# Two layers of attention and feed-forward on one core: experts and router in one PSUM bank, three banks for maxima, chains cut into pieces, experts' rows built later

## The chip, the cores and the metric

One core of a Trainium2 chip runs the whole program. TensorE (PE), VectorE (DVE), ScalarE (ACT), GpSimd (POOL) and SyncE (SP, which here issues nearly all DMAs) each run their own list of instructions in order and wait for one another by semaphores. The metric is the device time of one execution in microseconds (us).

## The reference

The input is four sequences ("batches" in the kernel) of 512 tokens by 128. Two layers are computed, each an attention and a feed-forward part with a residual sum and a layer norm behind each.

- First attention: 16 heads of 8, each split into two half heads with a softmax of their own; `a = a1 - lam * a2`, out = `a @ v`, an RMS norm, then `@ wo`.
- First feed-forward: `silu(gate) * up`, then down, where every matmul's inputs are quantised to FP4 in blocks of 16 (block maximum / 6 as scale).
- Second attention: 16 query heads and 4 key heads of 64 with rotary positions, causal.
- Second feed-forward: a router picks one of 8 experts for each token; the expert is `relu(x @ W1 + b1) @ W2 + b2`, scaled by the router's weight.

## The kernel before

The four batches are pipelined. `attention1(r)` is the second attention of batch r, and `overlap(r)` runs three things beside each other: the first attention of batch r+1, the first feed-forward of batch r, and the experts of batch r-1. The order is start, overlap(-1), attention1(-1), overlap(0), attention1(0), overlap(1), and so on to overlap(4). In overlap(3) and overlap(4) there is no first attention left; `alone(i)` says so of the experts of batches 2 and 3.

The order of the work is written out by hand. An overlap walks over slots (s, c) with c from 0 to 3, and in each slot every engine does the same list: scores of the first attention, maxima, feed-forward, experts. The tables at the top (`UP`, `DOWN1`, `SORTED_TURN`, `HID_TURN`, `DOWN`, `O0_TURN`) say which piece stands in which slot. Every engine's list is fixed, so a wait holds all that stands behind it on that engine.

The first attention has two passes. In the first, PE computes two tiles of scores per slot into banks for maxima, and DVE reduces each (L895) and frees the bank. This pass runs 13 slots ahead of the second (`A_LEAD`). When a group of 16 maxima is there, POOL splits it into three parts, PE transposes them (L1416), DVE copies the row (L901), and SP sends it into three rows of `qst` (`max_row0`, L412). In the second pass PE computes two score tiles (L1435), which include the maxima through these rows, ACT takes the exponentials (L1160), and PE multiplies by the values (L1452). The scores of slots (s, 0) with even s wait for the row of group s / 2.

PSUM has eight banks. Banks 0 and 1 hold scores, 2 and 3 maxima, 4 the first attention's output, 7 the feed-forward and transposes. Banks 5 and 6 are added to scores and maxima in overlap(-1) and overlap(0), and are the experts' and the router's in overlap(1) and overlap(2).

The experts' stream: layer norm (`centre`, `scale`), transposes, router, `place_tokens` (which slot each token goes to, and which expert each of 11 tiles has), a scatter to HBM by POOL (L567), a fetch of the sorted rows by SP (L420) beside the experts' weights (L429), transposes (L1328), then for each tile up (L1346), relu (L1117), down (L1356) and a copy (L1122); a store, a gather by POOL (L573), and the last sum.

The weights are fetched from `expert_rows`, a copy in HBM that the kernel makes itself, with W1, W2 and b1 of an expert side by side; its nine DMAs are among `loads` (L357), which SP issues before overlap(-1). The quantisation of the feed-forward starts with `block_max`, `block_scale`, `over_scale` and `powers` on DVE and goes on with four steps on POOL (`quantise`, L546; L551 is the first, L560 the last). SP's order within an overlap is:

```
for g in range(NG):
    if r + 1 < BATCH:
        max_row0(r + 1, g)
    if 1 <= r:
        for j in WEIGHTS_AFTER.get(g, ()):
            fetch_expert(r - 1, j)      # j == 0 waits for tiles_ready
        if g == 1:
            fetch_sorted(r - 1)         # waits for the scatter
```

Of the kernel before, what the change touches and what calls it, by code (L numbers as in the profile page):

```python
# [17 lines left out]
P = 128  # L18
# [56 lines left out]
SLOTS = len(MAX_SLOT) + len(ROW_SLOT)  # L75

# [6 lines left out]
HID_TURN = {(5, 0): 0, (6, 0): 1, (7, 0): 2, (8, 0): 3}  # L83
HID_KEEP = {(5, 1): 0, (6, 1): 1, (7, 1): 2, (8, 1): 3}
DOWN = {(5, 2): 0, (6, 2): 1, (7, 2): 2, (8, 2): 3}
DOWN_KEEP = {(5, 3): 0, (6, 3): 1, (7, 3): 2, (8, 3): 3}
# [13 lines left out]
SORTED_TURN = {(3, 2): 0, (3, 3): 1, (4, 0): 2}  # L100
UP, DOWN_LAG, DOWN1 = {}, (2, 4), ({}, {})
for _n in range(2 * NTILE):
    _at = 17 + 43 * _n // (2 * NTILE)
    UP.setdefault((_at // 4, _at % 4), []).append((_n // 2, _n % 2))
    if _n % 2:
        for _lag, _table in zip(DOWN_LAG, DOWN1):
            _table[(_at + _lag) // 4, (_at + _lag) % 4] = _n // 2
# [5 lines left out]

def expert_banks(i, j):

    return (5, 6, 6) if not alone(i) else (2 * (j % 2), 2 * (j % 2) + 1, 5 + j % 2)
# [31 lines left out]
def banks0(r):  # L148

    return {-1: ((0, 1, 5), (2, 3, 6)), 0: ((0, 1, 6), (2, 3, 5))}.get(r, ((0, 1), (2, 3)))  # L150


def build(nc, x, w_qkv, wo, lq1, lq2, lk1, lk2, norm_w, w_gate, w_up, w_down,
# [8 lines left out]
    with ExitStack() as ctx:  # L162
# [127 lines left out]
        first_in, ffn_in, qk_in, weights_in = sem("first_in"), sem("ffn_in"), sem("qk_in"), sem("weights_in")  # L290
        setup_act, setup_pe, setup_dve, setup_pool = sem("setup_act"), sem("setup_pe"), sem("setup_dve"), sem("setup_pool")
# [52 lines left out]
        def _(sp):  # L344
# [8 lines left out]
            for i, v in enumerate((lq1, lk1, lq2, lk2)):  # L353
# [9 lines left out]
                (expert_rows[:, :, 0:FF1], W1),  # L363
                (sorted_x.rearrange("(t p) d -> p t d", p=P), nothing.rearrange("p (t d) -> p t d", t=NTILE)),
                (b2_sb[:, :], b2),
            ]
            for c in range(FF1 // P):
                loads.append((expert_rows[:, :, FF1 + E * c:FF1 + E * (c + 1)], W2.rearrange("e (c p) d -> c e p d", p=P)[c]))
                loads.append((expert_rows[:, :, WROW - FF1 // P + c:WROW - FF1 // P + c + 1],
                              b1.rearrange("e (c p a) -> c e p a", p=P, a=1)[c]))  # L370
# [110 lines left out]
        def _(pool):  # L481
# [64 lines left out]
            def quantise(a, c, n, done):  # L546
# [29 lines left out]
            def overlap(r):  # L576
# [4 lines left out]
                for g in range(NG):  # L581
# [4 lines left out]
                    if hidden and g in (2, 3):  # L586
                        if g == 2:
                            pool.wait_ge(hs_ready, r + 1)
                        next(rounds)
                        next(rounds)  # L590
# [3 lines left out]
            def turn(k, nx, v, rounds):  # L594

                if k < BATCH and 25 <= v < 29:
                    if v == 25:
# [33 lines left out]
        def _(dve):  # L631
# [125 lines left out]

            def over_scale(src, a, n, at=0):
# [6 lines left out]
            def place_tokens(i):  # L765

                count = ps[:, 5, NT * NE + NT * NE:NT * NE + NT * NE + NE]
                ranks = ps[:, 5, NT * NE:2 * NT * NE].rearrange("p (t n) -> p t n", t=NT)
# [4 lines left out]
                dve.wait_ge(ranks_ready, i + 1)  # L773
                step(dve.tensor_tensor(over, count.rearrange("p (e a) -> p e a", a=1).broadcast_to([P, NE, NT]),
                                       full_at.rearrange("p (a m) -> p a m", a=1).broadcast_to([P, NE, NT]), ALU.is_gt)); settle()
                step(dve.tensor_reduce(n_tiles, over, AX, ALU.add)); settle()
                step(dve.tensor_tensor(under, along(n_tiles, NE), tiles_under, ALU.mult)); settle()
                step(dve.tensor_reduce(base, under, AX, ALU.add)); settle()
                step(dve.tensor_tensor(rank_at, ranks, along(base, NT), ALU.add)); settle()
                step(dve.tensor_tensor(rank_at, rank_at, OH, ALU.mult)); settle()  # L780
                step(dve.tensor_reduce(slot_f, rank_at, AX, ALU.add)); settle()
                dve.tensor_copy(slot, slot_f).then_inc(slots_ready, 1)
                step(dve.scalar_tensor_tensor(ends, n_tiles, float(P), base, ALU.mult, ALU.add)); settle()
                step(dve.tensor_tensor(past, along(ends, NTILE), tile_at.rearrange("p (t a) -> p t a", a=1).broadcast_to([P, NTILE, NE]),
                                       ALU.is_le)); settle()
                step(dve.tensor_reduce(tile_f, past, AX, ALU.add)); settle()
                dve.tensor_scalar(tile_expert, tile_f, NE - 1.0, None, ALU.min).then_inc(tiles_ready, 1)

            def experts_stream(s, c, i):

                if (s, c) == (-1, 0):
# [3 lines left out]
                    dve.tensor_tensor(ZC[:, :, :], X[:, :, :], tiles(5), ALU.add).then_inc(att1_sum, 1)  # L795
                    dve.wait_ge(att1_sum, i + 1)
# [5 lines left out]
                if (s, c) == (0, 2):  # L802
                    dve.wait_ge(xc_turned, i + 1)
                    dve.tensor_copy(xTC[:, :], ps[:, 5, :]).then_inc(xTC_ready, 1)
                    centre(XP, bnC, mvC, varC)
                if (s, c) == (1, 0):
                    dve.wait_ge(logits_ready, i + 1)
                    step(dve.tensor_tensor(L, ps[:, 5, 0:NT * NE].rearrange("p (t n) -> p t n", t=NT), every(br_sb[:, :]), ALU.add)); settle()
                    step(dve.tensor_reduce(top, L, AX, ALU.max)); settle()
                    step(dve.tensor_tensor(IS, L, each(top), ALU.is_equal))  # L810
                    dve.tensor_tensor(OG, L, each(top), ALU.subtract).then_inc(lc_ready, 1); settle()
# [12 lines left out]
                if (s, c) == (2, 2):  # L824
                    dve.wait_ge(oh_turned, i + 1)
                    dve.tensor_copy(ohT, ps[0:NE, 5, :]).then_inc(ohT_ready, 1)
                    dve.wait_ge(oh_ready, i + 1)
                if (s, c) in SORTED_TURN:
# [3 lines left out]
                    dve.tensor_scalar(xsT[:, 4 * P * b:4 * P * b + w], ps[:, 5 + b % 2, 0:w], lng[:, 0:1], lng[:, 1:2],  # L832
# [21 lines left out]
            def ffn_stream(s, c, r):  # L854
# [4 lines left out]
                if (s, c) in ((0, 1), (0, 2)):  # L859
                    if c == 1:  # L860
                        dve.wait_ge(hid_done, NT * (r + 1))
                        dve.wait_ge(xq_ready, r + 1)
                    block_max(part(hl, c - 1), 704, 44 * (c - 1))
                if (s, c) == (0, 3):
                    block_scale(1408)
                if (s, c) in ((1, 0), (1, 1)):
                    settle()
                    step(over_scale(part(hl, c), part(ha, c), 704, 44 * c))
# [784 lines left out]
```

## Time and profile before

| | |
|---|---|
| median of 3 runs | 1362.13 us (1359.47 to 1363.06) |
| profiled execution | 1364.12 us, span from first to last instruction 1362.3 us |
| granted TensorE clock, mean | 0.823 |
| PE busy | 1040.2 us (76%) |
| DVE busy | 778.9 us (57%) |
| ACT busy | 646.9 us (47%) |
| POOL busy | 451.1 us (33%) |

Times within the profile count from the span's start. Busy shares are means over stages that differ; a stage is read by its own window. "idle before <-X" in a row is the time for which the engine stood idle ahead of that instruction, and what ended it. The granted clock is a share of 2.4 GHz.

### The profile page before, as it was taken

Reading aid. Unit: us, or ns where it says so; the run is one execution under the profiler, and the core shown is the slowest. Engines: PE = TensorE matmul, PEld = TensorE weight load, DVE = VectorE, ACT = ScalarE, POOL = GpSimd, SP = SyncE. Lnnn points to the kernel's source line nnn. Section 1 sums busy time; section 2 is a strip of 40 time slices with the busy share of each in tenths; the row PEclk is TensorE's granted clock in tenths of the full one; section 3 lists DMA queues with packets and bytes.
Section 4 is the critical chain, followed back from the end, with each engine's and each line's share of the span. In section 5 each row is a group of like instructions: output and inputs, shape, how many; then the busy total and the mean of one; then the engine's idle time right before and its main releaser. Section 6 shows DMA issues by size and latency. Waiting matters only on the chain. (4 is left out here: it accounts for less than half of the span.)

```text
span 1362.3 us, 20051 instructions
## 1 busy us (share of the span) xinstructions
PE 1040.2 (76%) x7121; PEld 538.4 (40%) x7121; DVE 778.9 (57%) x1809; ACT 646.9 (47%) x1581; POOL 451.1 (33%) x520
## 2 busy tenths in 40 slices
PE   2458837788998867789889866889888836799845
PEld 1012321233455432444445441444445526445534
DVE  4458447774777566463677656564487541376431
ACT  1057712577266233577266423577347513246414
POOL 3000020400677203200477503200376622278411
PEclk7569965789999665889999875799999967899957
DMA  5710030000012003100103002200100014100042
GB/s 140 188 30 3 10 101 0 2 2 10 1 47 55 0 1 122 49 17 23 40 1 102 1 1 77 94 18 17 38 1 1 1 56 144 37 1 1 1 168 68
DMA packets 54305, 56.83 MB, mean 42 GB/s; under 512 B 13688, under 2 KB 46016, under 8 KB 53440
## 3 DMA queue, kind: packets, MB, share of 16 engines
q1 hardware_dynamic: 53184, 53.47, 13.6%
q0 software_dynamic: 1024, 2.10, 0.5%
q8 instruction: 57, 0.93, 0.3%
q14 instruction: 40, 0.33, 0.1%
HBM read 43.16 MB, written 16.20 MB: 44 GB/s over the span
## 5 line engine op out<-in xcount | busy, mean ns | idle before, releaser
L895 DVE TENSOR_REDUCE mx<-ps 128x1 f32<-128x512 f32 x512 | 323.7, 684 | 156.5 <-PE ps L1410 153.4
L1160 ACT ACTIVATE PROB<-ps 128x512 f32<-128x512 f32 x512 | 276.1, 600 | 196.3 <-PE ps L1435 193.7
L538 POOL TENSOR_SCALAR PROB<-PROB,rsum 128x128 f32<-128x128 f32 (+3 forms) x224 | 229.0, 1035 | 62.0 <-DVE rsum L1023 61.6
L1202 ACT ACTIVATE PROB<-ps,mx 128x128 f32<-128x128 f32 (+3 forms) x256 | 133.1, 526 | 156.5 <-DVE mx L1018 154.3
L1410 PE MATMUL ps<-kst,qst 24*128 24x512 bf16 x512 | 170.0, 478 | 39.8 <-DVE mx L895 25.7
L1435 PE MATMUL ps<-qst,kst 27*128 27x512 bf16 x512 | 143.4, 445 | 53.5 <-DMA qst<-mrow 31.1
L519 POOL CAST mparts<-mx 128x16 bf16<-128x16 f32 x32 | 6.3, 197 | 526.7 <-DVE mx L895 526.7
L1452 PE MATMUL ps<-PROB,v 128*32 128x256 f32 x2048 | 175.4, 434 | 3.0 <-ACT OREG L1169 2.7
L1018 DVE TENSOR_REDUCE mx<-ps 128x1 f32<-128x128 f32 (+3 forms) x256 | 113.1, 483 | 72.9 <-PE ps L1497 72.9
L1514 PE MATMUL ps<-cst,PROB 128*128 128x128 f32 x640 | 114.1, 301 | 32.5 <-POOL PROB L538 11.4
L1494 PE MATMUL ps<-MREG,QREG 64*128 64x384 f32 (+3 forms) x512 | 107.4, 497 | 0.0
L1435 PEld LDWEIGHTS ps<-qst,kst 27*128 27x128 bf16 x512 | 32.8, 93 | 185.1 <-ACT PROB L1160 86.0
L1514 PEld LDWEIGHTS ps<-cst,PROB 128*128 128x128 f32 x640 | 75.2, 149 | 61.4 <-issue 22.9
L1117 ACT ACTIVATE MREG<-ps,wexp 128x128 f32<-128x128 f32 x176 | 53.9, 368 | 84.7 <-PE ps L1346 84.7
L1011 DVE SCALAR_TENSOR_TENSOR RREG<-ps,bqk,rope_sb 128x512 f32<-128x512 f32 x96 | 67.7, 746 | 21.1 <-PE ps L1479 21.1
L1524 PE MATMUL ps<-PROB,MREG 128*64 128x256 f32 (+3 forms) x512 | 77.5, 445 | 0.7 <-DVE PROB L1031 0.7
L1410 PEld LDWEIGHTS ps<-kst,qst 24*128 24x128 bf16 x512 | 37.5, 94 | 99.3 <-DVE mx L895 77.9
L1217 ACT COPY PROB<-ps 128x128 f32<-128x128 f32 (+3 forms) x128 | 54.4, 425 | 43.3 <-PE ps L1514 43.1
L1452 PEld LDWEIGHTS ps<-PROB,v 128*32 128x32 f32 x2048 | 47.6, 115 | 58.8 <-issue 41.0
L1031 DVE COPY PROB<-ps 128x128 f32<-128x128 f32 (+3 forms) x128 | 60.8, 475 | 11.3 <-PE ps L1514 10.7
L1479 PE MATMUL ps<-xT,wq_sb 128*128 128x512 f32 x128 | 61.2, 605 | 0.9 <-DVE MREG L1045 0.9
L1346 PE MATMUL ps<-PROB,wexp 128*128 128x128 f32 x352 | 60.1, 308 | 1.9 <-DVE PROB L832 1.9
(210 smaller groups left out, 1376.8 us busy)
## 6 DMA issues: line engine op xcount, KB each, us to landing
wexp<-expert_rows SPq DMA_DIRECT2D x44, 514.0 KB, 4.8
qk_terms<-RREG SPq DMA_DIRECT2D x48, 128.0 KB, 2.1
kst<-qk_terms SPq DMA_DIRECT2D x16, 192.0 KB
qst<-qk_terms SPq DMA_DIRECT2D x16, 192.0 KB
RREG<-sorted_x SPq DMA_DIRECT2D x4, 704.0 KB, 4.7
sorted_y<-RREG SPq DMA_DIRECT2D x4, 704.0 KB, 3.9
expert_rows<-in_L_ffn_W_dram SPq DMA_DIRECT2D x1, 2048.0 KB
expert_rows<-in_L_ffn_W_dram SPq DMA_DIRECT2D x4, 512.0 KB
```

The source lines that it names most:

```text
L538: pool.tensor_scalar(tile, tile, rsum1[:, 2 * v + half:2 * v + half + 1], None, ALU.mult).then_inc(scaled1, 1)
L895: dve.tensor_reduce(mx0[:, ga % 2, col:col + 1], ps[:, max_banks[MAX_SLOT[n] % len(max_banks)], :], AX, ALU.max, negate=True).then_inc(slo ...
L1011: dve.scalar_tensor_tensor(ropeT[:, i % 2, u], ps[:, banks[u], :], bqk[:, u, c:c + 1], rope_sb[:, u], ALU.add, ALU.mult).then_inc(rope_rea ...
L1018: dve.tensor_reduce(mx1[:, col:col + 1], ps[:, a1_bank(v, half), 0:P * (v % 4 + 1)], AX, ALU.max, negate=True).then_inc(max1_done, 1)
L1160: act.activation(prob0[:, s % 2, q % 4, q % 8 // 4], ps[:, s0_banks[q % len(s0_banks)], :], ACT.Exp, scale=float(HD0) ** -0.5).then_inc(ex ...
L1202: act.activation(prob1[:, half, at:at + w], ps[:, a1_bank(v, half), 0:w], ACT.Exp, bias=mx1[:, col:col + 1], accum_out=sum1[:, col:col + 1 ...
L1410: pe.matmul(ps[:, max_banks[at % nm], :], qst[rows, n // 16, P * qt:P * (qt + 1)], kst[rows, n // 16, :], start=True, stop=True).then_inc( ...
L1435: pe.matmul(ps[:, s0_banks[q % ns], :], kst[rows, g, P * kt:P * (kt + 1)], qst[rows, g, :], start=True, stop=True).then_inc(s0_ready, 1)
L1452: ins = pe.matmul(ps[32 * j:32 * j + 32, 4, qs], v0[:, kt, 4 * j + m // 4, :], prob0[:, m % 2, j, u // 2, qs], start=(m % 2 == 0 and u == ...
L1494: pe.matmul(dst[i], qT[half(i), w, P * qt:P * (qt + 1)], k1[half(i), g, 0:n], start=True, stop=False)
L1514: ins = pe.transpose(ps[:, 4 + i, P * kt:P * (kt + 1)], prob1[:, i, at + P * kt:at + P * (kt + 1)], ident)
L1524: ins = pe.matmul(ps[64 * h:64 * h + 64, 6, P * kt:T], v1[:, kt, D1 * (w // 2):D1 * (w // 2 + 1)], probT[:, w % 2, h, (TSTEP + P) * kt:(TS ...
```

## The change

In overlap(1) and overlap(2) the router and the experts use bank 6 alone, and bank 5 is a third bank for the maxima from the 19th on (`LEAD`). An expert tile takes three slots: both halves of up and half of the relus in the first, the other relus in the second, down and the copy in the third. The sorted rows' transposes go through bank 6 one group after another. The DVE chains of the router and of the quantisation, which stood in slots (0,1) to (2,2), are cut into pieces, at most one in a slot, up to (4,3); what hangs on them moves (sorted transposes from (3,2) to (5,0), first tile from (4,1) to (6,2), feed-forward transposes from (5,0) to (6,2), the transpose of X from (10,0) to (14,2)). The first of POOL's four quantisation steps becomes a DVE step (`shifts`). The nine DMAs that build `expert_rows` are issued after the term loads of overlap(-1), with a semaphore of their own that SP awaits before overlap(1). The loads of the second attention's q and k weights go behind the first term loads.

```diff
-HID_TURN = {(5, 0): 0, (6, 0): 1, (7, 0): 2, (8, 0): 3}
+HID_TURN = {(6, 2): 0, (7, 2): 1, (8, 2): 2, (9, 2): 3}
...
-SORTED_TURN = {(3, 2): 0, (3, 3): 1, (4, 0): 2}
-UP, DOWN_LAG, DOWN1 = {}, (2, 4), ({}, {})
+SORTED_TURN = {(5, 0): 0, (5, 2): 1, (6, 0): 2}
+UP, DOWN1 = {}, {}
 for _n in range(2 * NTILE):
-    _at = 17 + 43 * _n // (2 * NTILE)
+    _at = 25 + 35 * _n // (2 * NTILE)
...
+def tile_at_slot(s, c, lead):
+    n = 4 * s + c - lead - 26
+    return n // 3 if n >= 0 and n % 3 == 0 and n // 3 < NTILE else None
...
+def max_bank(k, at):
+    if k >= 2 and at < LEAD:
+        return 2 + at % 2
+    return (2, 3, 6 if k == 0 else 5)[at % 3]
...
-            for dst, src in qk_loads:
-                sp.dma_start(dst, src, allow_slow_non_contiguous=True).then_inc(qk_in, 16)
             n_loads[:] = [len(ffn_loads), len(qk_loads), len(loads)]
             store_parts(0)
             load_terms(0)
+            for dst, src in qk_loads:
+                sp.dma_start(dst, src, allow_slow_non_contiguous=True).then_inc(qk_in, 16)
...
                 if r == 1:
                     sp.wait_ge(weights_in, 16 * n_loads[2])
+                    sp.wait_ge(experts_in, 16 * len(expert_loads))
...
                     fetch_again(r + 2)
+                if r == -1:
+                    for dst, src in expert_loads:
+                        sp.dma_start(dst, src, allow_slow_non_contiguous=True).then_inc(experts_in, 16)
...
-                step(pool.tensor_scalar(c, c, 1.0, 1.5 * 2.0 ** 22, ALU.max, ALU.mult))
-                yield
-                settle()
                 step(pool.tensor_tensor(a, a, c, ALU.add))
...
+            def shifts(c):
+                return dve.tensor_scalar(c, c, 1.0, 1.5 * 2.0 ** 22, ALU.max, ALU.mult)
...
-                if (s, c) == (1, 2):
+                if (s, c) == (2, 1):
                     scale(XP, ZC, mvC, stC, stdC, 3 * i + 2, lnC)
-                    place_tokens(i)
-                if (s, c) == (1, 3):
+                if (s, c) in ((2, 3), (3, 1), (3, 3)):
+                    place_tokens(i, 2 * s + c // 2 - 5)
+                if (s, c) == (4, 1):
...
-                if (s, c) in ((0, 1), (0, 2)):
+                if (s, c) in ((0, 0), (0, 2)):
...
-                if (s, c) in ((1, 2), (1, 3)):
+                if (s, c) in ((2, 2), (3, 0)):
                     settle()
-                    ins = powers(part(ha, c - 2), part(hc, c - 2))
+                    step(powers(part(ha, s - 2), part(hc, s - 2)))
+                if (s, c) in ((3, 2), (4, 0)):
+                    settle()
+                    ins = shifts(part(hc, s - 3))
...
+                    j = tile_at_slot(s, c, 0)
+                    if j is not None:
+                        n = NTILE * i + j
+                        if j == 0:
+                            pe.wait_ge(xe_ready, 3 * (i + 1))
+                        else:
+                            pe.wait_ge(y_kept, n)
                         pe.wait_ge(wexp_in[n % RING], 16 * (n // RING + 1))
...
+                        up(i, j, 0, 6, 0)
+                        up(i, j, 1, 6, 0).then_inc(up_ready, 2)
+                    j = tile_at_slot(s, c, 2)
+                    if j is not None:
+                        n = NTILE * i + j
+                        pe.wait_ge(relu_done, 4 * (n + 1))
+                        down(n, ps[:, 6, 0:P]).then_inc(down1, 1)
...
-                if (s, c) == (10, 0):
+                if (s, c) == (14, 2):
                     pe.wait_ge(lnB, 2 * r + 2)
+                    if r + 1 < BATCH:
+                        pe.wait_ge(o0_kept, NG * (r + 1) + 6)
                     transpose_tiles(X, 7, x_turned)
```

`place_tokens` keeps its instructions; its piece 1 ends with the slots and its piece 2 with the tiles' experts.

## Rows read from the trace of the kernel before

**Rows 1.** Windows: stretch and length, engines' busy us, clock, DMA share, GB/s.

```profile
0.00:80.20 80.20, 22.99 (x52) 7.84 (x52) 30.99 (x59) 4.68 (x9) 12.50 (x44) 0.60 0.63 151
25.90:28.80 2.90, 2.08 (x9) 1.65 (x9) 2.69 (x12) 1.44 (x4) 0.00 (x0) 0.50 0.40 136
40.00:54.00 14.00, 11.97 (x22) 2.01 (x22) 12.11 (x21) 0.00 (x0) 0.83 (x4) 0.50 1.03 293
54.00:80.20 26.20, 2.20 (x5) 0.51 (x5) 3.72 (x7) 0.00 (x0) 0.00 (x0) 0.50 0.43 86
492.70:654.00 161.30, 132.21 (x1048) 63.62 (x1049) 88.03 (x190) 98.81 (x209) 27.14 (x40) 0.79 0.15 49
```

**Rows 2.** SP in order of time, the start: start, us, what.

```profile
10.65 0.43 SPq L458 DMA_DIRECT2D wq_sb<-in_L_attn_Wq_dram  x1
...
19.04 7.67 SPq L401 DMA_DIRECT2D qk_terms<-RREG  x12
28.24 1.54 SPq L410 DMA_DIRECT2D kst<-qk_terms  x4
...
73.94 5.18 SPq L415 DMA_DIRECT2D qst<-mrow  x3
```

**Rows 3.** PE and DVE in order of time, the start.

```profile
41.20 0.61 PE L1410 MATMUL ps<-kst,qst 24*128 24x512 bf16 x3 [13.11 <-DMA qst<-qk_terms]
...
55.05 0.20 DVE L901 COPY mrow<-ps 48x128 bf16<-48x128 bf16 x1
...
80.25 0.60 PE L1435 MATMUL ps<-qst,kst 27*128 27x512 bf16 x2 [23.67 <-DMA qst<-mrow]
```

**Rows 4.** Windows of overlap(1): slots (0,0), (4,0), (6,2) on.

```profile
492.70:541.90 49.20, 34.41 (x189) 10.78 (x189) 35.73 (x89) 22.13 (x38) 13.89 (x14) 0.50 0.21 66
541.90:569.50 27.60, 21.20 (x177) 11.68 (x173) 13.15 (x23) 14.79 (x35) 6.53 (x6) 0.81 0.25 86
569.50:646.00 76.50, 68.70 (x606) 36.49 (x607) 38.16 (x78) 57.41 (x131) 3.32 (x16) 0.96 0.06 18
```

**Rows 5.** Waits of PE in overlap(1): us in total, times, longest.

```profile
PE ps L1416 <- DVE mx L895: 7.0, 6, 2.3
```

**Rows 6.** POOL and PE in order of time, overlap(0) at slot (5,0).

```profile
259.32 3.15 POOL L557 TENSOR_TENSOR QREG<-QREG 128x1408 f32<-128x1408 f32 x1
262.54 2.58 POOL L560 TENSOR_TENSOR QREG<-QREG,q_sc 128x1408 f32<-128x1408 f32 x1
265.18 0.90 PE L1385 MATMUL ps<-cst,QREG 128*128 128x128 f32 x3 [5.78 <-POOL QREG L560]
```

**Rows 7.** DMA issues on the page: count, KB each, median us to landing.

```profile
wexp<-expert_rows SPq DMA_DIRECT2D x44, 514.0 KB, 4.8
```

**Rows 8.** All engines in order of time, before overlap(0)'s first score.

```profile
188.19 1.55 SPq L410 DMA_DIRECT2D kst<-qk_terms  x4
...
190.94 1.94 POOL L551 TENSOR_SCALAR ZB<-ZB 128x512 f32<-128x512 f32 x1 [9.71 <-DVE ZB L763]
...
224.81 1.79 SPq L415 DMA_DIRECT2D qst<-mrow  x3
...
227.74 0.60 PE L1435 MATMUL ps<-qst,kst 27*128 27x512 bf16 x2 [1.62 <-DMA qst<-mrow]
```

**Rows 9.** DVE and SP in order of time, overlap(1).

```profile
516.52 0.17 DVE L787 TENSOR_SCALAR tile_expert<-tile_f 128x11 int32<-128x11 f32 x1
517.81 3.02 SPq L429 DMA_DIRECT2D wexp<-expert_rows  x3
...
533.02 1.80 SPq L415 DMA_DIRECT2D qst<-mrow  x3
538.57 2.57 SPq L429 DMA_DIRECT2D wexp<-expert_rows  x3
```

**Rows 10.** PE in order of time: after overlap(1), and in overlap(3).

```profile
659.02 2.90 PE L1479 MATMUL ps<-xT,wk_sb 128*128 128x512 f32 x3 [4.17 <-DVE oall L916]
...
1156.54 0.93 PE L1291 MATMUL ps<-cst,X 128*128 128x128 f32 x4 [2.35 <-DVE X L737]
```

More of the change, by code:

```diff
@@ L145, in a1_bank, with score_banks, max_before @@
     return 2 * (v % 2) + half
-def banks0(r):
-    return {-1: ((0, 1, 5), (2, 3, 6)), 0: ((0, 1, 6), (2, 3, 5))}.get(r, ((0, 1), (2, 3)))
+def score_banks(r):
+    return {-1: (0, 1, 5), 0: (0, 1, 6)}.get(r, (0, 1))
+def max_bank(k, at):
+    if k >= 2 and at < LEAD:
+        return 2 + at % 2
+    return (2, 3, 6 if k == 0 else 5)[at % 3]
+def max_before(k, at):
+    for n in range(at - 1, -1, -1):
+        if max_bank(k, n) == max_bank(k, at):
+            return n
+    return None
 def build(nc, x, w_qkv, wo, lq1, lq2, lk1, lk2, norm_w, w_gate, w_up, w_down,
@@ L589, in overlap @@
                         next(rounds)
+                    if hidden and g == 3:
                         next(rounds)
@@ L594, in turn @@
             def turn(k, nx, v, rounds):
-                if k < BATCH and 25 <= v < 29:
-                    if v == 25:
+                if k < BATCH and 26 <= v < 29:
+                    if v == 26:
                         pool.wait_ge(xs_ready, k + 1)
@@ L778, in place_tokens @@
[L778 to L787, printed above, removed]
+                if piece == 0:
+                    dve.wait_ge(ranks_ready, i + 1)
+                    step(dve.tensor_tensor(over, count.rearrange("p (e a) -> p e a", a=1).broadcast_to([P, NE, NT]),
+                                           full_at.rearrange("p (a m) -> p a m", a=1).broadcast_to([P, NE, NT]), ALU.is_gt)); settle()
+                    step(dve.tensor_reduce(n_tiles, over, AX, ALU.add)); settle()
+                    step(dve.tensor_tensor(under, along(n_tiles, NE), tiles_under, ALU.mult)); settle()
+                    step(dve.tensor_reduce(base, under, AX, ALU.add))
+                elif piece == 1:
+                    settle()
+                    step(dve.tensor_tensor(rank_at, ranks, along(base, NT), ALU.add)); settle()
+                    step(dve.tensor_tensor(rank_at, rank_at, OH, ALU.mult)); settle()
+                    step(dve.tensor_reduce(slot_f, rank_at, AX, ALU.add)); settle()
+                    dve.tensor_copy(slot, slot_f).then_inc(slots_ready, 1)
+                else:
+                    settle()
+                    step(dve.scalar_tensor_tensor(ends, n_tiles, float(P), base, ALU.mult, ALU.add)); settle()
+                    step(dve.tensor_tensor(past, along(ends, NTILE), tile_at.rearrange("p (t a) -> p t a", a=1).broadcast_to([P, NTILE, NE]),
+                                           ALU.is_le)); settle()
+                    step(dve.tensor_reduce(tile_f, past, AX, ALU.add)); settle()
+                    dve.tensor_scalar(tile_expert, tile_f, NE - 1.0, None, ALU.min).then_inc(tiles_ready, 1)
@@ L985, in input0 @@
                     step(over_scale(rows(XA[:, :, :]), XQ[:, :], T)); settle()
-                    powers(XQ[:, :], rows(ZB[:, :, :])).then_inc(xs_ready, 1)
+                    step(powers(XQ[:, :], rows(ZB[:, :, :])))
+                if v == 25:
+                    settle()
+                    shifts(rows(ZB[:, :, :])).then_inc(xs_ready, 1)
             def turn(k, nx, v):
@@ L1292, in transpose_tiles, with up, down @@
                 ins.then_inc(done, 1)
+            def up(i, j, h, bank, at):
+                for f in (2 * h, 2 * h + 1):
+                    ins = pe.matmul(ps[:, bank, P * f - at:P * f - at + P], wexp[:, (NTILE * i + j) % RING, P * f:P * (f + 1)],
+                                    xsT[:, P * j:P * (j + 1)], start=True, stop=True)
+                return ins
+            def down(n, dst):
+                for f in range(4):
+                    ins = pe.matmul(dst, hE[:, n % 2, f, :], wexp[:, n % RING, FF1 + E * f:FF1 + E * (f + 1)],
+                                    start=(f == 0), stop=(f == 3))
+                return ins
             def experts_stream(s, c, i):
-                if (s, c) == (0, 1):
+                if (s, c) == (0, 0):
                     pe.wait_ge(lnC, 3 * i + 1)
-                    transpose_tiles(XP, 5, xc_turned)
+                    transpose_tiles(XP, RB, xc_turned)
                 if (s, c) == (0, 3):
@@ L1324, in experts_stream @@
                         pe.wait_ge(xs_in, 16 * (i + 1))
-                    if b == 2:
-                        pe.wait_ge(xe_ready, 3 * i + 1)
+                    if b and not alone(i) or b == 2:
+                        pe.wait_ge(xe_ready, 3 * i + (1 if alone(i) else b))
                     for t in range(4 * b, min(4 * b + 4, NTILE)):
-                        ins = pe.transpose(ps[:, 5 + b % 2, P * (t % 4):P * (t % 4) + P], xs[:, t], ident)
+                        ins = pe.transpose(ps[:, sorted_bank(i, b), P * (t % 4):P * (t % 4) + P], xs[:, t], ident)
@@ L1462, in overlap @@
                             if g == 0 and r >= 0:
+                                pe.wait_ge(ffn_sum, NT * (r + 1))
+                            if g == 6 and r >= 0:
                                 pe.wait_ge(xT_ready, 2 * r + 2)
```

211 lines of the change are left out of this document (113 added, 98 removed).

## The prediction

> **What bounds it now.** The views were read in this order: busy time by stages, SP's queue, PE's order of time, the waits. The chain of waits is of little use here: it breaks off at 1156 us. No engine is full; the time lies in waits of in-order queues, each with one place.
>
> The first place is the start. [rows 1] show 80.2 us with PE busy for 23.0. SP issues the twelve stores of the q and k parts from 19.04 and loads them again from 28.24; then come the other loads and the experts' rows, and only at 73.94 can it issue the first row of maxima [rows 2]. DVE had copied that row at 55.05; PE waits 23.67 us for it, until 80.25 [rows 3].
>
> The second place is overlap(1), 161.3 us for 64 slots with DVE busy for 88.0 [rows 1]; overlap(2) repeats it. [rows 4] split it: slots (0,0) to (3,3) take 49.2 us at a granted clock of 0.50, which is 1.2 GHz, with DVE busy 35.7; (4,0) to (6,1) take 27.6, (6,2) to (15,1) 76.5 with PE busy 68.7. The first stretch is long because DVE's chains stand in clumps between maxima that PE needs freed. In the second, slot (5,0) waits for POOL's quantisation, as it does in overlap(0) for 5.78 us [rows 6].
>
> **Part 1, the start.** Thirteen loads leave the place ahead of the stores. These begin at 10.65 instead of 19.04 at the earliest [rows 2], a little later because POOL must have made the parts, so the term loads, which took 13.0 us (28.24 to 41.20, [rows 2, 3]), land about 7 us earlier, at 34. But the thirteen now stand behind them, and DVE's set-up needs them before its first maximum. Their issue (8.4 us) hides behind the term loads; their landing does not: 0.7 MB at the 293 GB/s of [rows 1] is 2.5, small pieces and latency add 3, so 40. Set-up is 2.7 [rows 1]; maxima start at 43, or at 46 if SP is held at the small pieces. I take 44.4 against 41.9 before: the 7 us are lost to the next thing that is late. The row's copy follows 13.2 later, at 57.6. SP has about twelve loads left and is free by then; in overlap(0) a row issued at 224.81 was used at 227.74 [rows 8], 2.9. Scores begin at 60.5 instead of 80.25: **-19.7**, ends -23 (set-up hidden) and -16 (SP still held).
>
> **Part 2, the experts' rows later.** SP now issues them behind the term loads of the next batch and ahead of overlap(0)'s first row of maxima (224.81, [rows 8]). In times of before: those term loads land at 188.19 + 13.0 = 201.2. At the start the rest took from 41.20 to 80.25, 39.0, of which 2.4 MB of other loads are 8.2 at 293 GB/s [rows 1]: 30.9. So the row is in at 232.1 instead of 227.7, +4.4. Below: 0 (the copy runs beside the term loads); above: +11 (all 39). I take **+5**, near the sum and a little towards the middle. It swallows a small gain: POOL's first quantisation step of 1.94 us in the serial stretch before overlap(0) [rows 8] becomes a DVE step, bounded by 0.2 (mean of the set-up's, [rows 1]) and 1.94; I take 0.5, but it is SP that is late there.
>
> The trace moved 293 GB/s while large loads ran (40 to 54 us) and 86 while the experts' small pieces ran (54 to 80) [rows 1]. Beside these rows stands the Trainium skill, "DMA: Bandwidth & Descriptors", section Specifications: about 358 GB/s of HBM for a core. By it 4.2 MB read and as much written are an estimated 23.4 us, the row would land in time, and the sum would be 5 lower, 1318. The trace does not reach that figure.
>
> **Part 3, quantisation in the overlaps.** POOL's four steps become three, and their user moves from (5,0) to (6,2). POOL gets its flag at (4,0): 2 for that slot, 3.2 for the first step, which is of the kind of L557, then after the parts at (4,2) its last two, 3.15 and 2.58 [rows 6], with gaps about 12. (6,2) is ten slots on; eleven slots of the lead took 13.85 (41.20 to 55.05, [rows 3]), 1.26 each, so 12.6. The wait goes: -5.8 in overlap(0), and -0.7 for slots behind it that ran at 1.2 GHz; DVE, which is the limit there, has two steps more at 0.5: **-5.5**. Ends -8 and -2. If the cover of 0.6 is gone, it costs what POOL is late, 1 or 2.
>
> **Part 4, overlap(1) and (2), each.** PE may run a slot ahead of DVE with the third bank, and the row transposes (7.0 us of waits, [rows 5]) look a bank further back. With DVE's chains in pieces, slots (0,0) to (3,3) are bounded by DVE: 35.7 less 2.8 that moves past (4,0), plus 0.5 for a new step and 2.6 of gaps, 36 us. Alone that is -13. But SP's order is unchanged: behind the second row of maxima it waits for the tiles' experts, issues three expert loads, waits for the scatter, fetches the sorted rows, and only then sends the third row, which PE's score at (4,0) needs. Before, the experts were known at 516.69, 25 us ahead of (4,0). Now they are known at the end of (3,3). From there [rows 9]: 1.1 to SP's first issue, 2.0 to the third, 4.8 to its landing (the median, [rows 7]), and for the sorted rows and the row behind them the 5.55 from 533.02 to 538.57, less 1 that runs beside the weights: 12.5. Behind that score stand PE's maxima, so DVE and ACT stop too. 36 + 12.5 = 48.5 against 49.2: **-0.7**, ends -8 and +8.
>
> From (4,0) ten slots without POOL's wait, at 2.0 since the sorted rows now pass one bank after another: 20 against 27.6, -7.6. From (6,2) on PE is the limit [rows 4]: eleven tiles instead of about nine (2 x 2.3) and 1.5 of the first layer more, four row waits of 1 less: +2. The last tile's copy comes two slots earlier, and PE idles 4.17 before the next stage for want of it [rows 10]: -3. Together -9 each, **-18**; ends -17 and +3 each.
>
> **Part 5, the rest.** In overlap(3) PE no longer waits 2.35 amid the tiles [rows 10], POOL is a step earlier, the slots are known 1 later: **-3**, ends -6 and +2. Overlap(4) and the second attentions do the same work: **0**, ends -1 and +2.
>
> Sum: -19.7 + 5 - 5.5 - 18 - 3 = -41.2. The profiled execution took 1364.12 (span 1362.3), so 1322.9. It lies 2 us above the median of 1362.13; I say **1323**.
>
> **Rivals.** (a) *SP is not late at (4,0)*: the row, a few KB, passes the weights, or DVE's pieces end sooner. For it: at 533.02 the row shared the queue with the sorted rows and was not far behind them. Each overlap gains some 11 more: 1301. (b) *The overlaps gain nothing*: PE's own order holds the early slots (34.4 us of work in 49.2 at half clock, [rows 4]), and what is won from (4,0) on is lost in the denser tile slots. Without the -18: 1341. (c) *The stall only moves*: the experts' rows cost overlap(0) what they cost the start, 20 instead of 5: 1338. Against it: 23 us lie between the landing of the terms (201.2) and the row (224.81), which the start had not. (d) *Slower*: the queue of rows at (4,0) takes the place of the waits removed. If slots (0,0) to (3,3) do not shrink, the 12.5 come on top, and if the fourth row is held in the same way by the next three expert loads, another 7. Two overlaps at +19.5 with -19.7 + 5 - 5.5 - 3 make +16: 1380. It decides from 11.6 each. Against it: the fourth row is copied five slots after (4,0), by when three loads (2.0 + 4.8) are in.
>
> **Chances.** Forecast 0.52, (a) 0.17, (b) 0.16, (c) 0.09, (d) 0.06. The range takes the forecast's ends, (a) and (b): 1299 to 1346. About 0.3% is what a measurement of this kernel tells from no change. Faster: all but (d) and tails of (b) and (c), 0.91; within it 0.04; slower 0.05.
>
> **What would show it.** Right: the first score near 60 us, with no expert copy ahead of its row; overlap(0)'s first score some 5 us after its maxima allow; no first-layer transpose waiting for POOL; in overlap(1) one wait of PE of 10 us or more for a row of maxima, behind three expert loads. Wrong: overlap(1) above 160 us, or a first score after 70.

## The result, and the profile after

The changed kernel takes 1311.87 us (median of 4 runs, 1310.01 to 1315.45), the kernel before in the same comparison 1362.6 (4 runs, 1359.47 to 1363.25): a ratio of 0.9635 [0.9609, 0.9661]. 1323 was forecast, so the time by itself lies no nearer to the forecast than to rival (a), 1301; the trace has to tell them apart. The profiled execution took 1311.07, its span is 1309.3 and its mean granted clock 0.826 (before 0.823).

Where the 53.0 us of span went is read from marks that both kernels have (TensorE's first or last score of an overlap, the end of a second attention), in us from the span's start. The last column puts the prediction's terms against the stretches.

| mark | before | after | ahead by | this stretch | forecast |
|---|---|---|---|---|---|
| first score of overlap(-1) | 80.2 | 58.1 | 22.1 | -22.1 | -19.7 |
| first score of overlap(0) | 227.7 | 210.4 | 17.3 | +4.8 | +5 |
| last score of overlap(0) | 334.2 | 308.8 | 25.4 | -8.1 | -5.5 |
| first score of overlap(1) | 492.7 | 462.6 | 30.1 | -4.7 | 0 |
| first score of overlap(2) | 806.9 | 766.6 | 40.3 | -10.2 | -9 |
| end of attention1(2) | 1095.2 | 1043.1 | 52.1 | -11.8 | -9 |
| start of attention1(3) | 1181.0 | 1125.5 | 55.5 | -3.4 | -3 |
| end | 1362.3 | 1309.3 | 53.0 | +2.5 | 0 |

Windows of the kernel after, columns as in [rows 1]: the start up to the first score; then overlap(1) from the score at (0,0) to that at (3,3), from there to (4,0), from there to (6,2), and from (6,2) to the last score. The two lines between are from the time in which the experts' rows are copied.

```profile
0.00:58.10 58.10, 22.35 (x52) 7.30 (x52) 31.87 (x59) 4.68 (x9) 12.49 (x44) 0.63 0.53 136
...
172.00:182.00 10.00, 4.19 (x9) 2.26 (x10) 0.68 (x2) 2.33 (x3) 3.58 (x3) 0.50 0.97 246
182.00:204.50 22.50, 18.57 (x38) 5.17 (x37) 15.29 (x27) 2.67 (x4) 0.83 (x4) 0.50 0.51 118
...
462.60:495.10 32.50, 27.01 (x165) 8.26 (x165) 30.66 (x77) 20.91 (x36) 2.30 (x9) 0.50 0.00 1
495.10:510.00 14.90, 1.70 (x16) 0.37 (x12) 3.19 (x8) 1.10 (x3) 3.66 (x4) 0.50 0.58 173
510.00:529.30 19.30, 16.53 (x136) 5.25 (x136) 16.38 (x28) 10.76 (x21) 9.69 (x7) 0.74 0.29 89
529.30:608.20 78.90, 73.63 (x669) 40.66 (x665) 38.65 (x79) 61.40 (x147) 5.30 (x18) 0.96 0.14 44
```

The score at (3,3) comes 32.5 us into overlap(1), where it came at 46.7 before; DVE is busy for 30.7 of them, so it is nearly full. Then for 14.9 us hardly an engine works, so that (4,0) comes at 47.4, against the 49.2 of [rows 4]. The stretch from (4,0) to (6,2), which held POOL's wait, fell from 27.6 to 19.3. The timeline of the same kernel (start, us, engine, line; idle time before it in brackets) answers [rows 2, 3, 8 and 9]:

```profile
21.87 1.55 SPq L438 DMA_DIRECT2D kst<-qk_terms  x4
...
33.75 0.61 PE L1497 MATMUL ps<-kst,qst 24*128 24x512 bf16 x3 [6.23 <-DMA qst<-qk_terms]
...
39.07 0.69 DVE L734 TENSOR_SCALAR wq_sb<-wq_sb 128x1024 f32<-128x1024 f32 x1 [13.67 <-DMA bqk<-in_L_attn_bk_dram]
...
41.76 13.25 DVE L941 TENSOR_REDUCE mx<-ps 128x1 f32<-128x512 f32 x22
...
55.16 81.55 SPq L443 DMA_DIRECT2D qst<-mrow  x24
58.12 0.61 PE L1522 MATMUL ps<-qst,kst 27*128 27x512 bf16 x2 [1.66 <-DMA qst<-mrow]
...
171.98 2.96 SPq L508 DMA_DIRECT2D expert_rows<-in_L_ffn_W_dram  x2
174.99 11.01 SPq L508 DMA_DIRECT2D expert_rows<-in_L_ffn_b_dram  x1
...
203.85 0.21 DVE L947 COPY mrow<-ps 48x128 bf16<-48x128 bf16 x1
...
204.55 4.76 SPq L443 DMA_DIRECT2D qst<-mrow  x3
...
210.44 0.61 PE L1522 MATMUL ps<-qst,kst 27*128 27x512 bf16 x2 [5.06 <-DMA qst<-mrow]
...
498.07 0.32 DVE L825 TENSOR_SCALAR tile_expert<-tile_f 128x11 int32<-128x11 f32 x1
499.50 3.07 SPq L457 DMA_DIRECT2D wexp<-expert_rows  x3
502.62 0.43 SPq L448 DMA_DIRECT2D RREG<-sorted_x  x1
503.09 2.33 SPq L443 DMA_DIRECT2D qst<-mrow  x3
...
510.04 0.61 PE L1522 MATMUL ps<-qst,kst 27*128 27x512 bf16 x2 [13.24 <-DMA qst<-mrow]
```

The row of maxima now goes out at 55.16, as soon as DVE has copied it, and no copy of experts' rows stands ahead of it. In overlap(1) the forecast's one long wait is there: the row of slot (4,0) leaves at 503.09, behind three weights and the sorted rows. PE's waits (us in total, times, longest), in overlap(1) and then in overlap(3):

```profile
PE ps L1522 <- DMA qst<-mrow: 13.8, 2, 13.2
...
PE ps L1407 <- DMA RREG<-sorted_x: 11.8, 1, 11.8
```

### The profile page after: what moved, and what is told of

It reads as the page before. It is cut to its first block, busy times and chain, and to the rows that moved or that the text cites. A ratio compares the mean times of both kernels' runs of the same rounds, so it can differ in the third digit from the quotient of the medians.

```text
span 1309.3 us, 20064 instructions
## 1 busy us (share of the span) xinstructions
PE 1027.1 (78%) x7121; PEld 525.3 (40%) x7121; DVE 784.8 (60%) x1821; ACT 642.1 (49%) x1581; POOL 424.7 (32%) x512
## 4 chain that ended last, share of the span: by engine, by line
PE 54%; DVE 18%; ACT 9%; issue 8%; DMA 4%; SPq 3%; POOL 3%; POOLq 0%; ACTq 0%; DVEq 0%
PE ps L1539 9%; DVE mx L941 8%; PE ps L1568 7%; PE ps L1522 6%; PE ps L1583 5%; PE ps L1603 4%; PE ps L1613 4%; PE ps L1369 3%; ACT PROB L1227 3%; PE ps L1676 3%; PE ps L1456 2%; PE ps L1363 2%; DMA qst<-mrow 2%; PE ps L1497 2%; PE ps L1554 1%
## 5 line engine op out<-in xcount | busy, mean ns | idle before, releaser
L1497 PE MATMUL ps<-kst,qst 24*128 24x512 bf16 x512 | 158.3, 479 | 39.0 <-DVE mx L941 27.4
L1539 PE MATMUL ps<-PROB,v 128*32 128x256 f32 x2048 | 183.3, 451 | 3.0 <-ACT OREG L1236 2.6
L1603 PE MATMUL ps<-cst,PROB 128*128 128x128 f32 x640 | 113.3, 298 | 30.1 <-ACT PROB L1284 9.8
L1497 PEld LDWEIGHTS ps<-kst,qst 24*128 24x128 bf16 x512 | 34.1, 94 | 88.9 <-DVE mx L941 69.3
L1080 DVE COPY PROB<-ps 128x128 f32<-128x128 f32 (+3 forms) x128 | 60.8, 475 | 10.6 <-PE ps L1603 10.2
L962 DVE COPY oall<-ps 128x144 f32<-128x144 f32 x32 | 9.7, 303 | 95.5 <-PE ps L1554 95.5
```

What stands on the lines that cost most here:

```text
L1497: pe.matmul(ps[:, max_bank(k, at), :], qst[rows, n // 16, P * qt:P * (qt + 1)], kst[rows, n // 16, :], start=True, stop=True).then_inc(slo ...
L1539: ins = pe.matmul(ps[32 * j:32 * j + 32, 4, qs], v0[:, kt, 4 * j + m // 4, :], prob0[:, m % 2, j, u // 2, qs], start=(m % 2 == 0 and u == ...
L1603: ins = pe.transpose(ps[:, 4 + i, P * kt:P * (kt + 1)], prob1[:, i, at + P * kt:at + P * (kt + 1)], ident)
```

## Experiments

Medians are compared with 1311.9 of the changed kernel; the kernel before gave 1362.7, 1367.4 and 1363.5 beside the three sets. A kernel's runs spread over 4 to 10 us, so small effects are read from slots of the traces.

**The two parts of the start.** `qk_first` puts the q and k loads back:

```diff
+            for dst, src in qk_loads: ...
             store_parts(0)
             load_terms(0)
-            for dst, src in qk_loads: ...
```

> The changed kernel with the loads of the second attention's q and k weights put back ahead of the first stores. In the changed kernel the first terms land at 33.7 us, but DVE waits for these loads until 39.1 and its first maximum starts at 41.8, as it did before (41.89). Theory: moving the loads gained nothing, because DVE's set-up waits for them in place of the terms; the first maximum stays at 42 (+-1), the first score at 58, the time within 2 us of 1312. Rival: the earlier terms are worth their 7 us all the same (the row of maxima goes out into a less busy queue); then the first score comes at 65 and the time is 1319.

1310.2 us (ratio 0.9613 [0.9589, 0.9637]); the first score is at 58.4. The terms come at 41.4 again and nothing is lost. So this part of the change is worth nothing, as theory said: the first maximum waited for the terms before, and now it waits for the loads that were moved behind them.

`rows_early` issues `expert_loads` ahead of the loop over the overlaps again, instead of after `overlap(-1)`.

> The changed kernel with the nine copies that build the experts' rows put back ahead of overlap(-1). Theory (steps 1 and 2 of the prediction): SP is held by them until about 76, so the first score comes at about 79 instead of 58 (+21), and overlap(0)'s first row is no longer late, which gives back 5: 1328 (1323 to 1333). Rival: the stall only moves, and costs overlap(0) what it costs the start: 1312, with the first score of overlap(0) no later than now (210).

1327.6 us (0.9722 [0.9693, 0.9751]): 15.7 slower. The first row leaves at 76.25 and the first score is at 82.8 (+24.6); from the term loads of overlap(0) to its first score it takes 37.3 us (193.6 to 230.9) instead of 42.1 (168.3 to 210.4), 4.8 given back. The rival is out. The whole gain of the start is this one move, and within the changed kernel its price is the 5 that theory gave.

**What a wait at the start still costs.** `start2` moves DVE's set-up of the q and k weights (a wait and eleven steps) from ahead of the first maximum to slot (12,0) of overlap(-1), the k weights land in a place of their own meanwhile, and `expert_loads` go out behind overlap(0), ahead of `store_parts`:

```diff
-            dve.wait_ge(qk_in, 16 * n_loads[1])
...
+                    if r == -1 and (s, c) == (12, 0):
+                        set_up_qk()
...
+                    if r == 0:
+                        for dst, src in expert_loads: ...
...
-        wk_in = PROB[:, 7168:7424]
+        wk_in = QREG[:, 3584:3840]
```

> The changed kernel with two things moved: DVE's set-up of the second attention's q and k weights from ahead of the first maximum to slot (12,0) of overlap(-1), and the nine copies of the experts' rows from ahead of overlap(0) to behind it. Theory: the first maximum follows the terms at 33.8 instead of 41.8, so the first score comes at 50 (-8); overlap(0)'s first row is no longer behind the copies, -2.6 from there; 1301 (1298 to 1304). Rival 1: something else is late at the start (ACT's or PE's set-up, SP's other loads until 46.3 ahead of the row): first score at 54 or later, 1305. Rival 2: the copies now hold up the second attention or the next terms: nothing gained there, 1304.

1304.0 us (0.9543 [0.9516, 0.9570]). The first score came at 51.1, 7.0 earlier, so nothing else was late. From the term loads to overlap(0)'s first score it took 36.6 us instead of 42.1, and the copies held up nothing behind overlap(0): from its last score to overlap(1)'s first it took 155.7 us, within the 151.9 to 156.7 of the runs with the copies ahead of it, so the second rival is out. But overlap(-1) itself took 92.5 us to its last score instead of 88.5: at (12,0) the set-up holds up maxima, and 4 us went there: from (12,0) to (13,0) it took 9.4 us instead of 5.5 (see `best4`).

**SP's order in overlap(1) and (2).** `row_first` sends the third row before SP waits for the tiles' experts:

```diff
-WEIGHTS_AFTER = {1: (0, 1, 2), 2: (3, 4, 5), 3: (6, 7, 8), 5: (9,), 6: (10,)}
+WEIGHTS_AFTER = {2: (0, 1, 2), 3: (3, 4, 5), 4: (6, 7, 8), 5: (9,), 6: (10,)}
...
+                        if g == 2:
+                            fetch_sorted(r - 1)
                         for j in WEIGHTS_AFTER.get(g, ()):
                             fetch_expert(r - 1, j)
-                        if g == 1:
-                            fetch_sorted(r - 1)
```

> The changed kernel with SP's order changed in overlap(1) and (2): the third row of maxima goes out before SP waits for the tiles' experts; the sorted rows and the experts' weights follow it. Theory: PE's wait of 15 us at slot (4,0) is SP's order alone; it goes, some 4 us come back at (5,0), where the sorted rows are then late: 11 less in each of the two overlaps, 1290 (1286 to 1296). Rival 1: the wait only moves to (5,0), since scatter and fetch end when they did; 2 to 4 us in each, 1306. Rival 2: behind the wait the engines had work stored up that they then do faster; the slots after it run slower by as much without it, 1312.

1281.8 us (0.9392 [0.9368, 0.9415]): 30 less, where 22 were expected. Slot (4,0) comes at 34.1 us of overlap(1) instead of 47.4 and no wait appears at (5,0); 11.2 and 10.8 are left at the last score of overlap(1) and (2). So far theory, and both rivals are out. The other 8 lie where no row is sent: overlap(3) became 4.1 shorter (from the end of attention1(2) to the start of attention1(3), 78.3 instead of 82.4) and the last stretch 3.6. There only the sorted rows' place ahead of the weights can act. In waits of PE in this kernel, overlap(3) and then overlap(4):

```profile
PE ps L1407 <- DMA RREG<-sorted_x: 8.1, 1, 8.1
...
PE ps L1407 <- DMA RREG<-sorted_x: 8.9, 1, 8.9
```

They were 11.8 and 12.2. `row_only` keeps the order of weights and sorted rows (`fetch_sorted` stays behind the weights, both after g == 2) and moves the row alone:

> The changed kernel with the third row of maxima ahead of the wait for the tiles' experts as in the run with the row first, but the sorted rows behind the three weights as in the changed kernel. Theory: two effects are mixed in the 30 us of the row-first run. The row's own place is worth 11 in each of overlap(1) and (2); the sorted rows' place ahead of the weights is worth the rest in overlap(3) and (4), where no row is sent: there PE's wait for the sorted rows was 11.8 and 12.2 and became 8.1 and 8.9. So here 22 of the 30: 1290 (1286 to 1294), with the waits in overlap(3) and (4) at 12 again; in overlap(1) the sorted rows may be late by up to 3 at (5,0). Rival: the weights ahead of the sorted rows cost nothing, the 30 are the row's: 1282.

1295.0 us (0.9508 [0.9477, 0.9540]), 17 of the 30 and 1 us outside theory's range. The waits in overlap(3) and (4) are 11.4 and 12.1 again; in overlap(1) the sorted rows are 2.0 late for the transposes at (5,0), and the last scores of overlap(1) and (2) come 4.6 and 0.7 later than in `row_first`. The rival is out: the row is worth a little over half, the sorted rows' place the rest. How weights delay sorted rows is seen in overlap(3), in time, first of the kernel after:

```profile
1063.62 2.61 SPq L457 DMA_DIRECT2D wexp<-expert_rows  x3
1065.54 0.96 POOL L596 DMA_INDIRECT sorted_x<-ZC,slot  x1 [0.30 <-issue]
1071.71 0.38 SPq L448 DMA_DIRECT2D RREG<-sorted_x  x1
```

and of `row_first`:

```profile
1046.32 0.97 POOL L596 DMA_INDIRECT sorted_x<-ZC,slot  x1 [0.30 <-issue]
1048.57 0.36 SPq L448 DMA_DIRECT2D RREG<-sorted_x  x1
1049.95 1.51 SPq L457 DMA_DIRECT2D wexp<-expert_rows  x2
```

With three weights on the way SP saw the scatter land 6.2 us after POOL's last issue, without them 2.3; in overlap(4) it was 5.5 and 2.3.

**The third bank and the pieces.** `two_banks` sets `LEAD = SLOTS`.

> The changed kernel, in which the maxima of overlap(1) and (2) use banks 2 and 3 alone, all the way (the freed bank 5 stays empty for them). Theory: from (-1,0) on each maximum and each row transpose waits for the bank two places back instead of three; the slots up to (3,3) are bounded by DVE's chains and end 0 to 3 us later, and the row transposes behind them wait about 1 us more, five times: 3 to 8 in each overlap, 1323 (1316 to 1328). Rival: the pieces alone were enough and the third bank does nothing, since PE is held by SP at (4,0) and by its own work after it: 1312.

1323.3 us (0.9696 [0.9655, 0.9737]): 11.4 slower. In overlap(1) and (2) slot (3,3) comes 2.1 later, (4,0) 1.4 and 2.9, the last score 6.7 and 4.7. So in overlap(1) the third bank is worth most behind (4,0), in overlap(2) more than half of it ahead. Row transposes wait for a maximum again ([rows 5] has 7.0), in overlap(1):

```profile
PE ps L1503 <- DVE mx L941: 5.2, 6, 1.2
```

The rival is out.

`clumped` stands on `row_first`, so that SP's wait hides nothing, and puts the chains back to (0,1) to (2,2):

```diff
-                if (s, c) in ((2, 3), (3, 1), (3, 3)):
-                    place_tokens(i, 2 * s + c // 2 - 5)
+                if (s, c) == (1, 2): ...
+                    for piece in range(3):
+                        place_tokens(i, piece)
...
-                if (s, c) == (2, 0):
+                if (s, c) == (1, 1):
                     pe.wait_ge(oh16_ready, i + 1)
```

> The kernel with the row of maxima first (1281.8) with DVE's and ACT's chains of router and quantisation, and PE's router steps, back in the slots (0,1) to (2,2) in which they stood before; the third bank, the tables of the later slots and SP's order stay. Theory (step 4): the clumps are what made the slots up to (3,3) long; (3,3) comes at 40 to 46 us of overlap(1) instead of 32.5, and about 9 of it stays to the end of the overlap, twice: 1300 (1292 to 1308). Rival: the third bank carries the clumps, since PE may run a slot further ahead; (3,3) at 34, 1283.

1289.3 us (0.9439 [0.9418, 0.9460]): 7.5 slower than `row_first`. Slot (3,3) is at 37.1 and 38.5 in overlap(1) and (2): 4.6 and 5.9 later, between theory (7.5 to 13.5) and rival (1.5). The last scores come 2.4 and 4.4 later, where theory had 9 each. Theory's size was wrong. `clumped2` undoes both:

> The row-first kernel (1281.8) with the chains back in their old slots and the maxima of overlap(1) and (2) on two banks: what the two runs before undid one by one, undone together. Slot (3,3) came at 46.7 us in the kernel before, 32.5 in the changed one, 34.6 with two banks, 37.1 and 38.5 with the chains clumped. Theory: a bank more is what lets PE run on while DVE works on a clump; without both, (3,3) comes at 43 to 47, more than the sum of the two losses (39.2), and some 10 of it stays to the end of each overlap on top of the banks' 6: 1310 (1302 to 1318). Rival: they add, (3,3) at 39 to 41, 1300. The kernel before had router and experts in two banks, here they have one, so its 46.7 needn't come back whole.

1304.0 us (0.9577 [0.9543, 0.9611]). Slot (3,3) is at 41.6 in both overlaps: 9.1 later than in `row_first`, where the single losses are 2.1 and 4.6 to 5.9. So there is an interplay, but of 1 to 2 us, not the 4 to 8 that theory gave it: the slots come nearer to the rival. And 41.6 is not the 46.7 of the kernel before. The missing 5.1 are in that kernel's trace, at slot (3,2), where PE needed the sorted rows:

```profile
537.29 1.09 PE L1328 MATMUL ps<-cst,RREG 128*128 128x128 f32 x4 [5.05 <-DMA RREG<-sorted_x]
```

The change moved these transposes to (5,0). So of the 14.2 us by which (3,3) came earlier, 9.1 are chains and bank and 5.1 this wait. That split holds to about 1 us: up to (3,2) the kernel before was 1.1 ahead of `clumped2` (39.0 and 40.1), and from there to (3,3) it took 7.7 instead of 1.5, the wait and the transposes themselves.

**POOL's step.** `pool_back` gives `shifts` back to POOL, as the first of its four steps.

> The changed kernel with the first quantisation step back on POOL (4.94 us in an overlap, 1.94 in the attention before it) and the two DVE steps gone; the transposes that wait for it stay at slot (6,2). In the changed kernel POOL's last step ends at 249.4 us and the first of these transposes starts at 252.4: 3.0 us of slack in overlap(0). Theory (step 3): the 4.94 don't fit into it. The parts of the row behind the first step come 4.9 later and the last step at 254: overlap(0) loses 2 to 5, the stretch before it about 1, overlap(1) and (2), whose ten slots take 20 us, nothing: 1316 (1313 to 1319). Rival 1: moving the transposes to (6,2) alone cured the wait: 1312. Rival 2: POOL's step is what mattered and its wait comes back in each overlap: 1322 or more.

1316.7 us, against a slower kernel before (0.9638 [0.9602, 0.9674]), so the times alone don't tell it from the changed kernel. The trace does. POOL and PE's waits in overlap(0) of this kernel:

```profile
240.81 4.94 POOL L583 TENSOR_SCALAR QREG<-QREG 128x1408 f32<-128x1408 f32 x1 [8.21 <-DVE QREG L797]
...
249.78 0.22 POOL L554 TENSOR_TENSOR mparts<-mrem,mparts 128x16 bf16<-128x16 f32 x1
```

```profile
PE ps L1498 <- POOL mparts L554: 4.2, 1, 4.2
```

The long step holds back the parts of the next row, which end 37.8 us behind the overlap's first score (212.2) instead of 33.2 (243.6 and 210.4), and PE waits 4.2 us for them; (5,2) comes 3.0 later, the last score 2.4. Overlap(1) and (2) lose nothing, and neither does the stretch ahead of overlap(0) (41.6 us from the term loads to the first score, 42.1 in the changed kernel), where theory had 1. Otherwise theory holds; the wait is at the row of maxima rather than at the quantised tile.

**Together.** `best3` is `row_first` and `start2`:

> The row of maxima first, DVE's set-up late, the experts' rows behind overlap(0), all three on the changed kernel. Theory: the three stand in different stages and add: 1281.8 - 8 - 2.6 = 1271 (1267 to 1275). Rival: the copies behind overlap(0) run into the first attention's later loads and take back what they gave: 1274 to 1278.

1273.6 us (0.9309 [0.9284, 0.9333]), inside theory's range: the stages add. `best4` moves the set-up from (12,0) to (15,1), behind the last maximum:

> The row first, the experts' rows behind overlap(0), DVE's set-up late, but at slot (15,1) of overlap(-1), behind the last maximum, instead of (12,0), where it stood among maxima and that overlap became 4 us longer. Theory: the 4 come back: 1269.5 (1266 to 1273). Rival: overlap(-1) became longer because its granted clock fell at another time, not for the set-up's place: 1273.5.

1271.2 us (median of 6, 1266.6 to 1276.4; 0.9329 [0.9299, 0.9359]). Overlap(-1) takes 86.0 us to its last score instead of 92.1, in the one profile of each; but the medians differ by 2.4 only, and by the ratios not at all. The set-up's place is shown in the slots ((12,0) to (13,0) 5.5 instead of 9.4), not in the time. It is 41 us faster than the changed kernel and 92 faster than the one before.

## Why the prediction was right

**Part 1, right, and 2.4 too small.** -19.7 was forecast, -22.1 came. Maxima started at 41.8, not at 44.4: the loads landed at 39.1 instead of the 40 to 43 of the forecast; the row then took 3.2 from its copy, near the 2.9 of [rows 8]. The 3 us for small pieces and latency, which the forecast took from no row, came out: from PE's first maximum, which the terms released (33.75), to the landing it was 5.3, where 5.5 was forecast. What gave the gain is SP being free (`rows_early`); the loads' move gave 0 (`qk_first`), which is the forecast's own 7 us lost to the next late thing.

**Part 2, right in its mechanism; that its number fits is luck.** +5 was forecast and the stretch has +4.8, but only 2.6 of that lie where the late row acts. From the term loads to the first score it became 2.6 us longer (39.5 to 42.1). The first maximum came 0.8 sooner behind the term loads (16.0 instead of 16.8); the row's copy followed the first maximum as before (19.6); and from the copy to the score it took 6.6 instead of 3.2, because SP came to the row only at 204.55 and the row then landed behind the copies. In the kernel before these were

```profile
205.01 0.61 PE L1410 MATMUL ps<-kst,qst 24*128 24x512 bf16 x3
...
224.59 0.20 DVE L901 COPY mrow<-ps 48x128 bf16<-48x128 bf16 x1
```

and in the changed kernel

```profile
168.31 1.55 SPq L438 DMA_DIRECT2D kst<-qk_terms  x4
...
184.28 0.61 PE L1497 MATMUL ps<-kst,qst 24*128 24x512 bf16 x3
```

In all eight traces with the copies in this place it took 41.1 to 42.9, so against the kernel before they cost 1.6 to 3.3. Taking them out of the changed kernel gives back more, 4.8 (`rows_early`) to 5.5 (`start2`). What the DVE step in POOL's place gave (0.5 forecast) is not shown: with the step back on POOL, `pool_back`, the stretch took 41.6.

The other 2.2 were lost ahead of the term loads, where overlap(-1) took 88.5 us to its last score instead of 85.5. The forecast had no term there. The granted clock was 0.56 from 82 to 90 us and 1.00 at the same slots before (104 to 112), and with these slots unchanged overlap(-1) took from 86.2 (`qk_first`, granted 0.91 over it) to 89.9 (`two_banks`, 0.84).

The rule weighed there, 358 GB/s for a core by the Trainium skill, "DMA: Bandwidth & Descriptors", section Specifications, would have had the row in time. The trace does not bear that out: SP came to the row 32.6 us after its first copy (171.98 to 204.55), where the estimate by that figure was 23.4. In that time 246 GB/s were moved up to 182 us and 118 from there on: 5.1 MB, with the 4.2 MB of copies among them, so a copied byte counts once in these figures, where the estimate counts it as read and as written.

**Part 3, right and 2.6 too small.** The wait of [rows 6] is gone; PE starts these transposes 3.0 us after POOL's end:

```profile
246.77 2.59 POOL L589 TENSOR_TENSOR QREG<-QREG,q_sc 128x1408 f32<-128x1408 f32 x1
...
252.42 0.55 PE L1470 MATMUL ps<-cst,QREG 128*128 128x128 f32 x3
```

Of the -8.1, 6.2 stand at (6,2), 41.4 us into overlap(0) instead of 47.6: that is the forecast's -5.5 nearly to size. From there to (12,0) it is 3.9 shorter at a granted clock of 0.95 (before 0.83), and from (12,0) on 2.0 longer at 0.90 (before 1.00); no run tells the clock's share in these from that of the pieces moved. `pool_back` shows that moving them was not enough by itself: POOL's long step would also have held up a row of maxima, which the forecast did not name.

**Part 4, right in its mechanism.** -9 each was forecast, -10.2 and -11.8 came in the stretches, -9.4 and -9.7 within the two overlaps. The slices in overlap(1): (4,0) came at 47.4 where 48.5 was forecast, 34.2 of slots (36 forecast; `row_first` has (4,0) at 34.1) and 13.2 of waiting for SP (12.5 forecast); (4,0) to (6,2) took 19.3 and not 20. From (6,2) to the last score it lost 0.7 (78.2 to 78.9; +2 forecast), and the idle time ahead of attention1(1) fell from the 4.17 of [rows 10] to 1.31 (-3 forecast), though the way from the last score to it became only 1.1 shorter (11.4 to 10.3). Rival (a) is out: the row, a few KB, did not pass the weights; issued at 503.09, it was in at 510.0, 6.9 later, where the row of overlap(0) before took 2.9 [rows 8]. Beside this stands the Trainium skill, "DMA: Bandwidth & Descriptors", section Queues, rings and completion order: each DMA engine takes the descriptors of a ring in order. The trace agrees.

One reading of this part was incomplete. It put the 49.2 us of [rows 4] down to clumps and freed banks; 5.1 of them were PE's wait for sorted rows at (3,2), which that window contains and the prediction did not list. And the clumps cost 5 to 6 us, with the bank 9.1.

**Part 5, right; two stages beside it moved.** Overlap(3) gave 3.4, and the 2.35 of [rows 10] are gone. Two terms had no part in the forecast: attention1(0) was 3.6 shorter and attention1(3) 2.1 longer, the first with the same instructions but for the quantisation step that went from POOL to DVE, the second with the same. Their windows, of the kernel before:

```profile
342.50:483.00 140.50, 125.86 (x716) 70.11 (x715) 92.13 (x218) 61.78 (x182) 83.47 (x81) 0.89 0.10 25
...
1181.00:1290.80 109.80, 101.85 (x656) 57.49 (x656) 68.24 (x175) 53.82 (x171) 72.38 (x69) 0.99 0.01 4
```

and after:

```profile
316.80:453.70 136.90, 122.67 (x716) 69.25 (x715) 92.12 (x220) 61.72 (x182) 81.72 (x80) 0.93 0.10 26
...
1125.50:1237.40 111.90, 104.26 (x656) 58.33 (x656) 68.27 (x175) 53.75 (x171) 72.35 (x69) 0.96 0.01 3
```

DVE's busy time is the same; PE's follows the granted clock (0.89 to 0.93, 0.99 to 0.96). With the same instructions attention1(0) took from 134.6 (`two_banks`, granted 0.94) to 140.0 (`qk_first`, 0.89) in the runs above, so one trace says little of it. Attention1(3) is another matter: in every trace with the change it took 111.3 to 112.0, granted 0.96 or 0.97, and 109.8 at 0.99 in the one trace before. The change may well have made that difference through the clock; what brings the clock down there is not shown.

So the 11.8 us beyond the forecast are, by the table, 2.4 at the start, 2.6 in overlap(0), 4.0 in overlap(1) and (2), 4.7 less 2.5 in the stretches of attention1(0) and (3), for which the forecast had nothing, and 0.6 in the rest. What carries the forecast is the wait of 13.2 us for a row behind three expert loads: with it rival (a) is out, to which the time alone lies as near.

## What to carry to other kernels

An in-order DMA issuer is an engine like the others: list what stands behind each of its waits, and send what the next step needs ahead of any wait for something later; here the order of three entries in one list was worth 30 us, 17 of them the row's own place, more than the start's gain. Moving a late thing forward gains only up to the next late thing, so look for that one (DVE's wait for the q and k loads) before moving the first. When a long stretch is put down to one cause, add up all its waits first: the 5.1 us at (3,2) stood in the profile.

## What the runs showed of the hardware

- Large loads on SP's queue delay POOL's scatter too: 6.2 us instead of 2.3 from its last issue until SP goes on, with three loads of 514 KB on the way. Beside this stands the Trainium skill, "DMA: Bandwidth & Descriptors", section Issuing engines are not separate DMA queues: DMAs of all engines run on the same DMA engines and interleave. The trace agrees.
- The time of one kernel mostly follows the mean granted clock: `clumped` took 1281.7 us at 0.837 and 1291.8 at 0.824, `clumped2` 1299.0 at 0.831 and 1306.9 at 0.819. That is as much as several parts of this change, so parts under 5 us were read in slots of the traces.
- One of SP's issues of the experts' biases held SP for 11.0 us (175.0 to 186.0), while the copies ahead of it ran; later ones took 1.7 to 2.5.
